# Edge network: who makes the remainders, who copies the selection matrices, and how the two halves of a sum are turned

## The chip, the cores and the metric

The kernel runs on one core of a Trainium2 chip. The metric is the device time of one execution in microseconds (us). The engines are named as the profile names them: PE is TensorE (PEld its weight loads), DVE is VectorE, ACT is ScalarE, POOL is GpSimd, SP issues most of the DMAs. Each has a queue of its own, works it off in order, and waits for the others by semaphores.

## What is computed

Four graph layers, each followed by a residual addition and a layer norm, on 3125 nodes with 64 features and 53125 edges (50000 drawn ones and a loop at each node). The change lies in the second layer, the edge network, whose reference is (cut):

```
row, col = edge_index[0], edge_index[1]
h = concatenate([x[row], edge_attr], axis=1)
h = relu(h @ W1 + b1)
h = h @ W2 + b2
agg = scatter_mean(h, col, x.shape[0])
g = relu(concatenate([x, agg], axis=1) @ W3 + b3)
return g @ W4 + b4
x = _layernorm(x + ...)
```

## The kernel before

The nodes are cut into 25 tiles of 125 (NT), and each tile of destinations has 26 blocks (SB) of 128 edge slots. For a tile the kernel needs the 128 hidden values of every edge, after the relu, summed by destination. That is the stage "edge2", the functions pe_edge2, act_edge2, dve_edge2, pool_edge2 and sp_edge2. It is walked in steps, 7 for each tile, so 175 (G7). A step treats 4 blocks, 512 columns; the seventh step of a tile (g = 6) treats the 2 that are left, 256 columns, and is "the short step". All engines run the same loop over steps, each in its own order:

- **PE** gathers the source nodes' part of the hidden values by multiplying with a selection matrix (L3022, 12 bf16 matmuls in a step, 6 in the short one; three pieces of bf16 stand for one fp32 value). Three steps later (LAG) it sums that step's hidden values by destination (L3035, 4 matmuls, 2 in the short step). Its moving operand has 256 columns: 128 of the rounded value and 128 of the remainder, so the sum comes out in two halves of 128 columns, in bank 4 or 5. Five steps after a tile's last step (LAG + TURN_SUM) it turns the tile's sum (L3043).
- **DVE** adds the edges' part to what PE gathered (L3216, out of PSUM into one of three buffers pre). It makes the selection matrix of the next tile once per tile, in step g = 1 (L3193, src_tables). It makes the remainder, the relu of pre less its rounded value, in the steps g = 1, 3, 5 (L3199, rest). Once a tile it adds the two halves of the sum (L3234, tensor_reduce into `both`), and one step later than the turn it scales the turned sum (L3242).
- **ACT** takes the relu and rounds it to the reduced fp32 that the sum matmul reads (L3144, into one of four act_two). In the steps whose remainder POOL makes it takes the same relu once more, not rounded, into `whole` (L3150).
- **POOL** subtracts the rounded from the whole value in the steps g = 0, 2, 4, 6 (L3109).
- hot_e holds the selection matrix by destination in the sum's format, four buffers. The copy into it is made by POOL in the steps 0, 2, 3, 4, 6 (L3099) and by ACT in the steps 1 and 5 (L3153).

PE waits before each sum for the copy, for ACT's relu, and for the remainder of that step. DVE waits before each addition for the gather. Between these steps lies work once for every four tiles (a chunk, CH = 4, seven in all): two matmuls at the hidden layer (L3053, L3054), the output layer (L3062), four transposes (L3071), the attention inputs (L3080), and on DVE the layer norm (L854 to L861, L928, L929), each at a fixed distance in steps.

The tables that say who does what are REST_BY_POOL and CAST_BY_ACT. SP reloads the inputs of a tile when the copies and the additions of the tile two before it are done.

Of the kernel before, what the change touches and what calls it, by code (L numbers as in the profile page):

```python
# [13 lines left out]
ACT = mybir.ActivationFunctionType  # L14
AX = mybir.AxisListType.X
# [5 lines left out]
HID = 128  # L21
# [4 lines left out]
NP_, NT = 125, 25  # L26
# [122 lines left out]
def build(nc, I, out):  # L149
# [23 lines left out]
    with ExitStack() as ctx:  # L173
# [4 lines left out]
        ident = sb("ident", [128, 128])  # L178
# [31 lines left out]
        y1 = sb("y1", [128, N + WIN])  # L210
# [94 lines left out]
        pre = [e2_at([128, 4 * HID]) for _ in range(2)]  # L305
        low_end, high_end = e1_at.at, e2_at.at
        pre.append(e2_at([128, 4 * HID]))
        whole = [y1[:, (13 + 4 * k) * HID:(17 + 4 * k) * HID] for k in range(2)]
        both = [y1[0:NP_, (11 + k) * HID:(12 + k) * HID] for k in range(2)]
        ln1_sq = y1[0:NP_, 0:13 * C].rearrange("p (i f) -> p i f", f=C)  # L310
        px_rest = [y1[0:NP_, 13 * C + 4 * HID * k:13 * C + 4 * HID * (k + 1)] for k in range(2)]
        m_act = [y1[:, k * CH * NP_:(k + 1) * CH * NP_] for k in range(2)]
# [119 lines left out]
        def bank(b, n=BANK, off=0):  # L432
            return ps[:, b * BANK + off:b * BANK + off + n]
# [6 lines left out]
        def sem(name):  # L440

            if name in sems:
                return sems[name]
            if name not in branch_sems:
                if len(branch_sems) == len(by_branch):
                    by_branch.append(ctx.enter_context(nc.semaphore(f"branch{len(by_branch)}")))
                branch_sems[name] = by_branch[len(branch_sems)]
            return branch_sems[name]
# [18 lines left out]
        V, A, M = nc.vector, nc.scalar.activation, nc.tensor.matmul  # L467
# [2352 lines left out]
        G7 = 7 * NT  # L2820
        LAG = 3
        TURN_SUM = 2
        REST_BY_POOL = (0, 2, 4, 6)
        CAST_BY_ACT = (1, 5)

        def hi(ap):

# [173 lines left out]
        def pe_edge2(pe):  # L3001
# [11 lines left out]
            for step in range(E_STEPS):  # L3013
                if step < G7:
                    d, g = divmod(step, 7)
# [10 lines left out]
                if LAG <= step < G7 + LAG:  # L3026
                    s = step - LAG
                    d, g = divmod(s, 7)
# [10 lines left out]
                d, at = divmod(step - LAG - TURN_SUM, 7)  # L3039
                if at == 0 and 1 <= d <= NT:  # L3040
                    d -= 1
                    pe.wait_ge(sem("both_added"), d + 1)
                    nc.tensor.transpose(bank(4 + d % 2, NP_, 2 * HID), both[d % 2], ident[0:NP_, 0:NP_])\  # L3043
                        .then_inc(sem("sum_turned"), 1)
                for c in range(NCH):
                    if step == hid_step(c):
                        to = bank(6, chunk(c) * NP_)
# [7 lines left out]
                    if step == hid_step(c) + OUT:  # L3055
# [5 lines left out]
                        for j, t in enumerate(tiles(c)):  # L3061
                            ins = M(bank(7, C, j * C)[0:NP_, :], m_act[c % 2][:, j * NP_:(j + 1) * NP_], w4[:, :],  # L3062
                                    start=True, stop=True, skip_group_check=True)
# [28 lines left out]
        def cast_hot(engine, op, s, name):  # L3092

            d, g = divmod(s, 7)
            js = groups(d)[g]
            engine.wait_ge(sem(f"hot_back{d % 2}"), hot_landed(d, 0))
            if s >= NE:
                engine.wait_ge(sem("act_summed"), s - NE + 1)
            op(hot_e[s % NE][:, 0:len(js), :], hot_in[d % 2][:, js[0]:js[0] + len(js), :]).then_inc(sem(name), 1)  # L3099
# [21 lines left out]
        def act_edge2(act):  # L3121
            act_px_mid(act, 0)
            act_back(act, 4)
            act_px_mid(act, 1)
            act_px_high(act, 2)
            ln1_root(act, 2)
            act_px_high(act, 3)
            act_back(act, 5)
            act_px_mid(act, 2)
            act_px_high(act, 4)  # L3130
            act_px_mid(act, 3)
            act_back(act, 6)
            for i in range(5, NCH):
                act_px_high(act, i)
                act_px_mid(act, i - 1)
            act_px_mid(act, NCH - 1)
            for step in range(E_STEPS):
                if step < G7:
                    d, g = divmod(step, 7)
                    m = HID * len(groups(d)[g])  # L3140
                    act.wait_ge(sem("e1_added"), step + 1)
                    if step >= 4:
                        act.wait_ge(sem("act_summed"), step - 3)
                    ins = A(act_two[step % 4][:, 0:m // HID, 0, :],  # L3144
                            pre[step % 3][:, 0:m].rearrange("p (k h) -> p k h", h=HID), ACT.Relu)
                    if g in REST_BY_POOL:
                        n = rests(step, True)
                        if n > 2:
                            act.wait_ge(sem("rest_pool"), n - 2)
                        ins = A(whole[n % 2][:, 0:m], pre[step % 3][:, 0:m], ACT.Relu)  # L3150
                    ins.then_inc(sem("act_relued"), 1)
                    if g in CAST_BY_ACT:
                        cast_hot(act, lambda to, of: A(to, of, ACT.Copy), step, "hot_act")  # L3153
                for c in range(NCH):
                    if step == hid_step(c) + 1:
                        act.wait_ge(sem("m_hid"), c + 1)
                        if c >= 2:
                            act.wait_ge(sem("m_out"), c - 1)
                        A(m_act[c % 2][:, 0:chunk(c) * NP_], bank(6, chunk(c) * NP_), ACT.Relu,
                          bias=prm[:, P_L1B3:P_L1B3 + 1]).then_inc(sem("m_relu"), 1)  # L3160
                    at = slice(c * CH, c * CH + chunk(c))
                    if step == hid_step(c) + ROOT:
                        ln_root(act, c, LN2 + c + 1)
                    if step == hid_step(c) + TURNED:
                        act.wait_ge(sem("back"), NCH + c + 1)
                        A(xt[:, cols(c)], bank(6, chunk(c) * NP_)[0:C, :], ACT.Copy).then_inc(sem("back_ev"), 1)
                    if step == hid_step(c) + HIGH:
                        act.wait_ge(sem("tab_mm"), NCH + c + 1)
                        A(p3[:, at, 0, :], hup_bank(c), ACT.Copy).then_inc(sem("tab_high"), 1)
                    if step == hid_step(c) + MID:  # L3170
                        act.wait_ge(sem("tab_left"), NCH + c + 1)
                        A(p3[:, at, 1, :], hup_left(c), ACT.Copy).then_inc(sem("tab_mid"), 1)

        def dve_edge2(dve, chain):
# [30 lines left out]
            for step in range(E_STEPS):  # L3205
                if step < G7:
                    d, g = divmod(step, 7)
# [15 lines left out]
                if step == 3:  # L3223
                    dve.wait_ge(sem("back_ev"), NCH)
                    V.tensor_tensor(xn[:, :, :], xn[:, :, :], b4b[:, :].unsqueeze(1).to_broadcast([NP_, NT, C]), ALU.add)\
                        .then_inc(sem("x_b4"), 1)
                d, at = divmod(step - LAG - 1, 7)
                if at == 0 and 1 <= d <= NT:
                    d -= 1
                    dve.wait_ge(sem("act_summed"), 7 * d + 7)  # L3230
                    if d >= 2:
                        dve.wait_ge(sem("sum_turned"), d - 1)
                    got = bank(4 + d % 2, 2 * HID)[0:NP_, :]
                    V.tensor_reduce(both[d % 2], got.rearrange("p (t h) -> p h t", t=2), AX, ALU.add).then_inc(sem("both_added"), 1)  # L3234
                d, at = divmod(step - LAG - TURN_SUM - 1, 7)
                if at == 0 and 1 <= d <= NT:
                    d -= 1
                    dve.wait_ge(sem("sum_turned"), d + 1)
                    c, k = divmod(d, CH)
# [10 lines left out]
                for c in range(NCH):  # L3250
                    if step == hid_step(c) + EVICT:
# [3 lines left out]
                        at = slice(c * CH, c * CH + chunk(c))  # L3255
# [4 lines left out]
                    at = slice(c * CH, c * CH + chunk(c))  # L3260
# [781 lines left out]
```

## Time and profile before

| | us |
|---|---|
| median of 3 runs | 1653.72 |
| lowest and highest | 1652.78, 1654.42 |
| profiled execution, its own time | 1656.8 |
| its span in the profile | 1655.0 |
| the stage that the change touches, from 765 to 1050 us | 285 |

The profiled execution was 3.1 us longer than the median. Between 0 and 765 us the edges are sorted and the first layer is computed; after 1050 us come the attention layer and the relation layer. Readings of a row "L3022 ... x12" are a run of 12 instructions with the time from the start of the first to the end of the last. Matmuls overlap and an instruction of DVE or ACT overlaps the next one at its end, so what an engine needs for one is the distance to the start of the next where it did not wait.

### The profile page before, as it was taken

What the parts mean: (1) busy time and instruction counts of PE and PEld (TensorE: products, weight loads), DVE (VectorE), ACT (ScalarE), POOL (GpSimd) and SP (SyncE); (2) the same over time, 40 slices, a digit from 0 to 9 for tenths busy, and PEclk for the clock granted to TensorE, in tenths of its full rate; (3) what the DMA queues carried; (4) which work ended last, traced back from release to release, by engine and by line L of the source; (5) the groups of instructions that cost most, each with busy time, mean ns of one, the idle gap of its engine ahead of it and who ended that gap; (6) DMA issues with size and microseconds to landing.
All of it is one profiled execution on the core that took longest, in us unless ns stands there. A gap on an engine that the chain in (4) does not pass through costs nothing.

```text
span 1655.0 us, 46737 instructions
## 1 busy us (share of the span) xinstructions
PE 1256.5 (76%) x19204; PEld 1134.4 (69%) x19205; DVE 1072.6 (65%) x2449; ACT 814.5 (49%) x2162; POOL 669.5 (40%) x733
## 2 busy tenths in 40 slices
PE   5764452626263689997988888789999989989896
PEld 2653342525252568996878777679999988889896
DVE  8333332425252543467878888688888878978886
ACT  5053442525252532115766666456666657555554
POOL 2777777777777700003878777200100100000000
PEclk9566665767666689997999999899999997999998
DMA  6935555747474858355878778466666503445442
GB/s 193 367 120 206 201 203 187 258 170 276 154 291 139 297 222 289 141 221 224 346 295 314 301 296 314 166 252 236 241 228 233 209 27 138 167 165 193 153 176 81
DMA packets 86125, 359.59 MB, mean 217 GB/s; under 512 B 23740, under 2 KB 35281, under 8 KB 78929
## 3 DMA queue, kind: packets, MB, share of 16 engines
q1 hardware_dynamic: 72594, 348.83, 57.2%
q0 software_dynamic: 13312, 7.69, 1.8%
q8 instruction: 155, 2.54, 0.6%
q14 instruction: 64, 0.52, 0.1%
HBM read 250.77 MB, written 105.68 MB: 215 GB/s over the span
## 4 chain that ended last, share of the span: by engine, by line
PE 35%; POOL 30%; DVE 15%; issue 14%; ACT 4%; DMA 1%; POOLq 0%; DVEq 0%; SPq 0%; ACTq 0%
POOL recs L2192 25%; PE ps L3706 8%; PE ps L2664 6%; PE ps L3352 6%; POOL rounded L3109 4%; PE ps L3720 3%; PE ps L3022 3%; PE ps L3035 2%; POOL rounded L3099 2%; DVE arena L3294 1%; DVE arena L3295 1%; PE ps L3408 1%; ACT arena L3424 1%; PE ps L3337 1%; DVE arena L673 1%
## 5 line engine op out<-in xcount | busy, mean ns | idle before, releaser
L2192 POOL DMA_INDIRECT recs<-arena x416 | 414.0, 995 | 160.3 <-issue 126.0
L2514 PE MATMUL ps<-ident,arena 128*128 128x128 f32 (+1 forms) x175 | 47.5, 419 | 240.6 <-DVE arena L2381 182.3
L2375 DVE TENSOR_TENSOR arena<-arena 128x25 f32<-128x25 int32 x25 | 5.0, 199 | 310.5 <-DMA arena<-recs 274.0
L2514 PEld LDWEIGHTS ps<-ident,arena 128*128 128x128 f32 (+1 forms) x175 | 32.4, 212 | 248.9 <-issue 242.6
L3706 PE MATMUL ps<-arena 125*128 125x64 bf16 x5850 | 192.2, 194 | 11.1 <-issue 10.9
L3706 PEld LDWEIGHTS ps<-arena 125*128 125x128 bf16 x5850 | 186.3, 98 | 13.8 <-issue 13.6
L3752 ACT ACTIVATE arena<-ps,arena 128x64 f32<-128x64 f32 x650 | 141.6, 334 | 102.8 <-PE ps L3720 102.6
L3099 POOL CAST rounded<-arena 128x512 fp32r<-128x512 bf16 (+1 forms) x125 | 95.1, 778 | 167.3 <-DMA arena<-hot_out 163.1
L3109 POOL TENSOR_TENSOR rounded<-y,rounded 128x512 fp32r<-128x512 f32 x100 | 130.2, 1302 | 75.9 <-ACT y L3150 75.8
L3144 ACT ACTIVATE rounded<-arena 128x512 fp32r<-128x512 f32 (+1 forms) x175 | 104.7, 598 | 98.2 <-DVE arena L3216 97.3
L3022 PE MATMUL ps<-arena 125*128 125x128 bf16 x1950 | 145.9, 227 | 4.2 <-DVE arena L3193 4.2
L3035 PE MATMUL ps<-rounded 128*128 128x256 f32 x650 | 124.2, 312 | 30.5 <-POOL rounded L3109 29.9
L3216 DVE TENSOR_TENSOR arena<-ps,arena 128x512 f32<-128x512 f32 (+1 forms) x175 | 112.5, 648 | 38.7 <-PE ps L3022 36.5
L3352 PE MATMUL ps<-arena,y 128*68 128x125 f32 x984 | 123.0, 276 | 10.3 <-ACT y L3434 5.0
L3022 PEld LDWEIGHTS ps<-arena 125*128 125x128 bf16 x1950 | 121.2, 103 | 13.6 <-issue 7.2
L2664 PE MATMUL ps<-agg,arena 125*128 125x193 bf16 (+1 forms) x1250 | 124.6, 253 | 5.3 <-DVE yn L2682 4.9
L2547 ACT ACTIVATE arena<-arena 128x832 f32<-128x832 f32 x25 | 22.4, 898 | 197.1 <-DMA arena<-recs 197.0
L3035 PEld LDWEIGHTS ps<-rounded 128*128 128x128 f32 x650 | 92.4, 198 | 36.0 <-issue 35.6
L3352 PEld LDWEIGHTS ps<-arena,y 128*68 128x68 f32 x984 | 107.2, 143 | 13.5 <-issue 13.1
L2664 PEld LDWEIGHTS ps<-agg,arena 125*128 125x128 bf16 x1250 | 107.6, 101 | 11.4 <-issue 9.9
L2584 ACT ACTIVATE arena<-ps 128x512 f32<-128x512 f32 (+1 forms) x192 | 83.8, 522 | 41.9 <-PE ps L2539 41.9
L2403 DVE TENSOR_TENSOR arena<-iota,iota_i 128x768 bf16<-128x768 bf16 (+1 forms) x150 | 99.8, 735 | 0.9
(392 smaller groups left out, 2717.8 us busy)
## 6 DMA issues: line engine op xcount, KB each, us to landing
arena<-ids_out SPq DMA_DIRECT2D x100, 832.0 KB, 6.4
arena<-hot_out SPq DMA_DIRECT2D x75, 832.0 KB, 4.8
arena<-e_out SPq DMA_DIRECT2D x25, 1664.0 KB, 8.6
arena<-adj_out SPq DMA_DIRECT2D x41, 800.0 KB, 7.9
e_out<-arena SPq DMA_DIRECT2D x25, 1024.0 KB
hot_out<-arena SPq DMA_DIRECT2D x25, 832.0 KB
adj_out<-arena SPq DMA_DIRECT2D x25, 800.0 KB
e_out<-arena SPq DMA_DIRECT2D x25, 640.0 KB
```

Of the source, the lines that this page charges most:

```text
L2192: nc.gpsimd.indirect_dma_start(out=recs, out_offset=bass.IndirectOffsetOnAxis(ap=slot_row[:, t:t + 1], axis=0), in_=rec_in[:, t, :], in_of ...
L2403: ins = V.tensor_tensor(to[d % 2][:, a:b, :].rearrange("p j (n t) -> p j n t", t=2), steps, twice[d % 2][:, kind, a:b, :].unsqueeze(2).to_ ...
L2664: ins = M(to, blocks[0:NP_, k, :], yp[l % 2][:, k, 0:PIECES * C + (l == 0)], start=k == 0, stop=k == NT - 1, skip_group_check=True)
L3022: ins = M(bank(step % 4, HID, k * HID), src_hot[d % 2][0:NP_, j * SLOTS:(j + 1) * SLOTS], px[:, block_of(d, j), piece, :], start=piece == ...
L3035: ins = M(bank(4 + d % 2, 2 * HID), hot_e[s % NE][:, k, :], act_two[s % 4][:, k, :, :].rearrange("p t h -> p (t h)"), start=j == 0, stop=j ...
L3099: op(hot_e[s % NE][:, 0:len(js), :], hot_in[d % 2][:, js[0]:js[0] + len(js), :]).then_inc(sem(name), 1)
L3109: nc.gpsimd.tensor_tensor(act_two[r % 4][:, 0:n, 1, :], whole[rests(r, True) % 2][:, 0:n * HID].rearrange("p (k h) -> p k h", h=HID), act_ ...
L3144: ins = A(act_two[step % 4][:, 0:m // HID, 0, :], pre[step % 3][:, 0:m].rearrange("p (k h) -> p k h", h=HID), ACT.Relu)
L3216: V.tensor_tensor(pre[step % 3][:, 0:m], bank(step % 4, m), e1_in[d % 2][:, 4 * g * HID:4 * g * HID + m], ALU.add).then_inc(sem("e1_added" ...
L3352: ins = M(bank(6 + d % 2, NP_)[0:ROW, :], xmsg[n % 3][:, k, :], hot32[(7 * d + j // 4) % NH][:, j % 4, 0:NP_], start=j == 0, stop=j == NT, ...
L3706: ins = M(bank(step % 4, C, k * C), hot_r[d % 2][r][0:NP_, j * SLOTS:(j + 1) * SLOTS], px3[:, block_of(d, j), piece, r * C:(r + 1) * C], s ...
L3752: ins = A(xrel[q % 3][:, 0, k, :], bank(q % 4, C, k * C), ACT.Copy, scale=w_all[:, d, j:j + 1])
```

## The change

REST_BY_POOL shrinks from the steps 0, 2, 4, 6 to step 6 alone, so DVE makes the remainder in the steps 0 to 5. CAST_BY_ACT goes from 1 and 5 to 0, 1, 3, 4, so POOL keeps the copies of the steps 2, 5 and 6. DVE no longer adds the two halves of a tile's sum; ACT copies both halves out of PSUM into `both`, now 256 wide, and PE turns each half by an ordinary fp32 matmul with the identity, the second one accumulating on the first. The buffers `whole` and `both` move within y1.

```
-        whole = [y1[:, (13 + 4 * k) * HID:(17 + 4 * k) * HID] for k in range(2)]
-        both = [y1[0:NP_, (11 + k) * HID:(12 + k) * HID] for k in range(2)]
+        whole = [y1[:, (16 + 4 * k) * HID:(20 + 4 * k) * HID] for k in range(2)]
+        both = [y1[0:NP_, (8 + 2 * k) * HID + 512:(10 + 2 * k) * HID + 512] for k in range(2)]
...
-        REST_BY_POOL = (0, 2, 4, 6)
-        CAST_BY_ACT = (1, 5)
+        REST_BY_POOL = (6,)
+        CAST_BY_ACT = (0, 1, 3, 4)
...
                     pe.wait_ge(sem("both_added"), d + 1)
-                    nc.tensor.transpose(bank(4 + d % 2, NP_, 2 * HID), both[d % 2], ident[0:NP_, 0:NP_])\
+                    to = bank(4 + d % 2, NP_, 2 * HID)
+                    M(to, both[d % 2][:, 0:HID], ident[0:NP_, 0:NP_], start=True, stop=False)
+                    M(to, both[d % 2][:, HID:2 * HID], ident[0:NP_, 0:NP_], start=False, stop=True)\
                         .then_inc(sem("sum_turned"), 1)
...
                     if g in CAST_BY_ACT:
                         cast_hot(act, lambda to, of: A(to, of, ACT.Copy), step, "hot_act")
+                d, at = divmod(step - LAG - 1, 7)
+                if at == 0 and 1 <= d <= NT:
+                    d -= 1
+                    act.wait_ge(sem("act_summed"), 7 * d + 7)
+                    if d >= 2:
+                        act.wait_ge(sem("sum_turned"), d - 1)
+                    A(both[d % 2], bank(4 + d % 2, 2 * HID)[0:NP_, :], ACT.Copy).then_inc(sem("both_added"), 1)
...
-                d, at = divmod(step - LAG - 1, 7)
-                if at == 0 and 1 <= d <= NT:
-                    d -= 1
-                    dve.wait_ge(sem("act_summed"), 7 * d + 7)
-                    if d >= 2:
-                        dve.wait_ge(sem("sum_turned"), d - 1)
-                    got = bank(4 + d % 2, 2 * HID)[0:NP_, :]
-                    V.tensor_reduce(both[d % 2], got.rearrange("p (t h) -> p h t", t=2), AX, ALU.add).then_inc(sem("both_added"), 1)
```

The engines' queues at the same places, first before, then after. In the changed kernel the line numbers are higher: on DVE L3225 is the addition of L3216, L3208 the remainder of L3199, L3202 the selection matrix of L3193, and L3243 the scaling of L3242.

PE before, from one turn on: the turn, then the gather of the short step.

```order
L3043 MATMUL ps<-ident,y 128x125
L3022 MATMUL ps<-arena 128x128 x6
L3035 MATMUL ps<-rounded 128x256 x4
L3022 MATMUL ps<-arena 128x128 x12
L3035 MATMUL ps<-rounded 128x256 x4
L3022 MATMUL ps<-arena 128x128 x12
```

PE after, at the same place:

```order
L3044 MATMUL ps<-ident,y 128x125
L3045 MATMUL ps<-ident,y 128x125
L3022 MATMUL ps<-arena 128x128 x6
L3035 MATMUL ps<-rounded 128x256 x4
L3022 MATMUL ps<-arena 128x128 x12
L3035 MATMUL ps<-rounded 128x256 x4
L3022 MATMUL ps<-arena 128x128 x12
```

The turn is two matmuls now, and the rest of PE's order stands.

DVE before, from the scaling of one tile's sum (in step 6) to the reduction of the next:

```order
L3242 TENSOR_TENSOR agg<-ps,arena 128x125
L3216 TENSOR_TENSOR arena<-ps,arena 128x512 x2
L3193 TENSOR_SCALAR arena<-arena,pidx_f 128x3328
L3216 TENSOR_TENSOR arena<-ps,arena 128x512
L3199 SCALAR_TENSOR_TENSOR rounded<-arena,rounded 128x4x128
L3216 TENSOR_TENSOR arena<-ps,arena 128x512 x2
L3199 SCALAR_TENSOR_TENSOR rounded<-arena,rounded 128x4x128
L3234 TENSOR_REDUCE y<-ps 125x128
```

DVE after, at the same place:

```order
L3243 TENSOR_TENSOR agg<-ps,arena 128x125
L3225 TENSOR_TENSOR arena<-ps,arena 128x512 x2
L3208 SCALAR_TENSOR_TENSOR rounded<-arena,rounded 128x4x128
L3202 TENSOR_SCALAR arena<-arena,pidx_f 128x3328
L3225 TENSOR_TENSOR arena<-ps,arena 128x512
L3208 SCALAR_TENSOR_TENSOR rounded<-arena,rounded 128x4x128
L3225 TENSOR_TENSOR arena<-ps,arena 128x512
L3208 SCALAR_TENSOR_TENSOR rounded<-arena,rounded 128x4x128
L3225 TENSOR_TENSOR arena<-ps,arena 128x512
L3208 SCALAR_TENSOR_TENSOR rounded<-arena,rounded 128x4x128
```

A remainder now follows every addition of 512 columns, one of them ahead of the selection matrix, and the reduction is gone.

ACT after, one tile from its step 0 on. L3146 is the relu, L3155 the copy, L3162 the new copy of the sum, L3152 the relu into whole.

```order
L3146 ACTIVATE rounded<-arena 128x4x128
L3155 ACTIVATE rounded<-arena 128x512
L3146 ACTIVATE rounded<-arena 128x4x128
L3155 ACTIVATE rounded<-arena 128x512
L3146 ACTIVATE rounded<-arena 128x4x128 x2
L3155 ACTIVATE rounded<-arena 128x512
L3146 ACTIVATE rounded<-arena 128x4x128
L3155 ACTIVATE rounded<-arena 128x512
L3162 ACTIVATE y<-ps 125x256
L3146 ACTIVATE rounded<-arena 128x4x128
L3146 ACTIVATE rounded<-arena 128x2x128
L3152 ACTIVATE y<-arena 128x256
```

The copy of the sum stands behind the relu and the copy of step 4; before, ACT had no part in it.

## Rows read from the trace of the kernel before

**Rows 1.** Windows: length, busy (count) of PE PEld DVE ACT POOL, PE clock, DMA.

```profile
765.00:1050.00 285.00, 246.26 (x2757) 223.07 (x2757) 240.34 (x391) 184.00 (x351) 219.46 (x224) 0.95 0.74 286
...
970.00:975.00 5.00, 1.98 (x27) 1.74 (x27) 4.96 (x8) 3.55 (x7) 3.18 (x3) 1.00 1.04 441
```

**Rows 2.** Waits from 790 to 1040 us: in total, times, longest.

```profile
DVE arena L3216 <- PE ps L3022: 32.0, 44, 2.1
...
PE ps L3035 <- POOL rounded L3109: 26.5, 25, 3.0
```

**Rows 3.** Groups by line and form, 765 to 1050 us: busy, mean ns | idle before.

```profile
L3199 DVE SCALAR_TENSOR_TENSOR rounded<-arena,rounded 128x512 fp32r<-128x512 f32 x75 | 70.7, 942 | 4.3 <-ACT rounded L3144 3.1
```

**Rows 4.** Timeline of DVE, the reductions that mark tiles: start, length, instruction.

```profile
898.00 0.41 DVE L3234 TENSOR_REDUCE y<-ps 125x128 f32<-125x256 f32 x1
907.71 0.41 DVE L3234 TENSOR_REDUCE y<-ps 125x128 f32<-125x256 f32 x1
...
953.09 0.41 DVE L3234 TENSOR_REDUCE y<-ps 125x128 f32<-125x256 f32 x1
```

**Rows 5.** Timeline of all engines, a quiet tile: one that has no chunk work.

```profile
898.46 0.33 PE L3043 MATMUL ps<-ident,y 125*128 125x125 f32 x1 [0.22 <-DVE y L3234]
...
898.62 0.50 PE L3022 MATMUL ps<-arena 125*128 125x128 bf16 x6
898.93 0.72 PE L3035 MATMUL ps<-rounded 128*128 128x256 f32 x4
...
899.49 0.84 PE L3022 MATMUL ps<-arena 125*128 125x128 bf16 x12
...
900.15 0.73 PE L3035 MATMUL ps<-rounded 128*128 128x256 f32 x4
...
901.60 0.69 DVE L3216 TENSOR_TENSOR arena<-ps,arena 128x512 f32<-128x512 f32 x1
...
902.21 1.08 DVE L3193 TENSOR_SCALAR arena<-arena,pidx_f 128x3328 bf16<-128x3328 f16 x1
902.33 0.63 ACT L3144 ACTIVATE rounded<-arena 128x512 fp32r<-128x512 f32 x1
902.45 1.96 POOL L3109 TENSOR_TENSOR rounded<-y,rounded 128x512 fp32r<-128x512 f32 x1 [0.53 <-ACT y L3150]
...
902.86 0.62 ACT L3153 ACTIVATE rounded<-arena 128x512 fp32r<-128x512 bf16 x1
...
903.20 0.69 DVE L3216 TENSOR_TENSOR arena<-ps,arena 128x512 f32<-128x512 f32 x1
903.80 1.16 DVE L3199 SCALAR_TENSOR_TENSOR rounded<-arena,rounded 128x512 fp32r<-128x512 f32 x1
```

**Rows 6.** Timeline, other places: a remainder alone, and a selection matrix beside a copy.

```profile
885.87 0.68 DVE L3199 SCALAR_TENSOR_TENSOR rounded<-arena,rounded 128x512 fp32r<-128x512 f32 x1
...
869.36 1.51 DVE L3193 TENSOR_SCALAR arena<-arena,pidx_f 128x3328 bf16<-128x3328 f16 x1
869.38 0.61 POOL L3099 CAST rounded<-arena 128x512 fp32r<-128x512 bf16 x1 [0.20 <-PE ps L3035]
```

**Rows 7.** Timeline of PE: ordinary fp32 matmuls, two records each.

```profile
894.84 0.99 PE L3080 MATMUL ps<-watt,xt_rows 66*125 66x74 f32 x8
```

**Rows 8.** The chain of work that ended last: chunk matmuls at the hidden layer.

```profile
866.10 1.11 PE ps L3053 x2
867.20 0.84 PE ps L3054 x2
```

**Rows 9.** Timeline of DVE, the middle of a chunk's layer norm.

```profile
877.83 0.41 DVE L857 TENSOR_TENSOR yn<-yn,stat 125x256 f32<-125x256 f32 x1
...
879.15 0.69 DVE L3216 TENSOR_TENSOR arena<-ps,arena 128x512 f32<-128x512 f32 x1
879.76 0.41 DVE L860 TENSOR_REDUCE stat<-y 125x4 f32<-125x256 f32 x1
...
880.31 0.69 DVE L3216 TENSOR_TENSOR arena<-ps,arena 128x512 f32<-128x512 f32 x1
```

## The prediction, before the changed kernel ran

> **What bounds the kernel now.** I read the windows first. In the 285 us of the stage from 765 to 1050 us PE is busy for 246.3 us, DVE for 240.3, POOL for 219.5 and ACT for 184.0 [rows 1]. No engine is full, so what counts is who waits for whom. The waits name a ring: from 790 to 1040 us PE waits 26.5 us for POOL's remainder before a sum, and DVE waits 32.0 us for PE's gather before an addition [rows 2]. A late remainder delays the sum, the sum delays the next gather behind it on PE, and the gather delays DVE. The timeline says what a tile takes: a quiet one 9.71 us (from the reduction at 898.00 to that at 907.71), four tiles with one chunk's work 45.38 us (907.71 to 953.09) [rows 4]. I therefore lay out one tile's longest loop after the change and compare it with these two numbers. Outside the stage nothing changes, and what lies behind it shifts with its end.
>
> **Prices.** They are distances from the start of one instruction to the next where nothing waited. PE: 12 gather matmuls 0.66 (899.49 to 900.15), 6 of them 0.31, 4 sum matmuls 0.56 (898.93 to 899.49), today's turn 0.16 [rows 5]; DVE sees a gather 0.84 us after its first matmul, about 0.89 with the semaphore. DVE: an addition 0.61 (901.60 to 902.21), the selection matrix 0.99 (902.21 to 903.20); ACT starts its relu 0.73 after the addition starts (901.60 to 902.33), and its next instruction 0.53 later [rows 5]. A remainder alone takes 0.68 us, as an addition does, so 0.60 to its successor [rows 6].
>
> **POOL's work moves to DVE.** For each tile DVE gets three more remainders of 512 columns, 75 in all, 75 x 0.60 = 45 us. It loses 25 reductions of 0.41 us each, about 0.33 in distance, 8 us. What gets cheaper is the waiting at POOL. The remainder that starts at 903.80 takes 1.16 us: POOL's subtraction, begun at 902.45, ends at 904.41, and 0.55 us later the remainder ends too [rows 5]. So a remainder stands until POOL is through. On average it takes 0.942 us [rows 3] against 0.68, so 75 x 0.26 = 20 us. DVE's busy time becomes 240 + 45 - 8 - 20 = 257 us, under the stage's length, but now the highest.
>
> The Trainium skill (SBUF — State Buffer, Who interferes with whom) states this as a rule: VectorE with two inputs in SBUF and GpSimd reading SBUF share a port pair that is locked for a whole instruction, and the later one blocks. The trace agrees, as just read. Taken as all that limits this stage, it gives the first rival below.
>
> **ACT** loses 75 whole relus of 512 columns and gains 50 copies of the same size and 25 copies of 256 columns out of PSUM, taken at 0.41 us (the reduction reads the same bank in that time [rows 4]). It stays near 180 of 285 us, so no load; but its new copy of the sum stands behind the relu and the copy of step 4, and PE's turn waits for it. Behind the turn stand the gather of the short step and everything after it.
>
> **The two turns.** The trace has no ordinary fp32 matmul of 125 columns. Eight records, four matmuls, of 74 columns took 0.99 us, 0.12 each [rows 7], and two records of 500 columns 0.84 us [rows 8], 0.42 each or 0.105 for 125 columns. So weight loading and issue set the pace, and I take four records at 0.12, 0.48 us. Below, it can't be less than two turns as they are now, 0.32; above, I take 0.75, an estimate: one and a half times the 0.12 for each record, for a first weight load that nothing hides and 125 columns in place of 74. No gain is possible here, since both matmuls do what one did.
>
> The Trainium skill speaks against this edit: TensorE: Matmul & The Clock Gate, Terms, calls transpose mode four times faster for fp32. By that the two ordinary matmuls would take 2 x 4 x 0.16 = 1.28 us, and the forecast would lie 25 x 0.8 = 20 us higher; the rows of ordinary matmuls in this trace speak for the smaller price.
>
> **The loop of a quiet tile after the change**, each item waiting for the one before it, with its g and ' for the next tile. On PE: the two turns 0.48, gather of g 6 0.31, sum of g 3 0.56, gather of 0' 0.66, sum of g 4 0.56, gather of 1' 0.89 until DVE starts: 3.46. On DVE: addition 1' 0.61, remainder 0' 0.60, selection matrix 0.99, addition 2', remainder 1', addition 3', remainder 2' 2.42, addition 4' 0.73 until ACT starts: 5.35. On ACT: relu 4' 0.53, copy 4' 0.53, copy of the sum 0.41 and its semaphore 0.05: 1.52. Together 10.33 us. One wait comes on top. POOL's copy for 2' becomes free when the sum of g 5 has run, 0.5 to 0.6 us after the addition 1' began, just when the remainder 0' has taken the port. The copy then goes next and the selection matrix waits for it. Rows 6 show that pair: begun together with a copy of 0.61 us, the matrix took 1.51 us in place of 1.08. I take 0.4, so 10.7 us against 9.7: **+1.0 us for a quiet tile**. The bounds of this wait are 0 and 0.61.
>
> Why not shorter, though POOL's subtractions are gone? Because PE now gets the sum one step later. Today DVE's reduction follows its remainder 3' at once and PE waits 0.22 us for it [rows 5]; then it will wait about 1.6 us in each tile: remainder 2' done, PE needs 0.56 for the sum of g 2', while ACT delivers the copy only 0.73 + 0.53 + 0.53 + 0.46 = 2.25 us after addition 4' began. Meanwhile DVE has queued work for 1.8 us and then stands until the gather of g 6 arrives.
>
> **Four tiles with a chunk.** On the loop lie, once per chunk, the hidden matmuls, 1.11 + 0.84 = 1.95 us [rows 8], between the sum of g 4 and the gather of 1'; the four transposes, 4 x 0.16 = 0.6 at most, I take 0.5; and part of the layer norm. That takes 1.32 us (877.83 to 879.15) and 0.55 (879.76 to 880.31) [rows 9] on DVE between additions 6 and 1'. From the end of the short gather's issue DVE then needs 0.2 until it sees it, then the short addition 0.34 and later the scaling 0.20 (both estimates, by their columns from the addition's 0.61), a remainder 0.60, the layer norm 1.32, addition 0' 0.61 and the norm's 0.55, in all 3.82, where PE needs 0.56 + 0.66 + 0.56 + 0.89 = 2.67: 1.15 more. Four tiles: 4 x 10.7 + 1.95 + 0.5 + 1.15 = 46.4 against 45.4, **+1.0 us**. It is less than four quiet tiles would lose, because today's chunk tiles lose time to POOL that comes back: PE is busy for only 1.98 of the 5 us from 970 to 975 [rows 1].
>
> **Sum.** The first three distances between tiles are quiet, 3 x 1.0 = 3 us; five groups of four follow, 5 x 1.0 = 5; the first tile and the last one, which only drain, about 1. Together +9 us. The profiled execution would go from 1656.8 to 1665.8; it stood 3.1 us over the median, so the median becomes **1662.7 us**, 0.5% slower. The edits' bounds: the port wait -10 to +5, the turns (0.32 and 0.75) -4 to +7, prices of the hand-laid chunks some 5 either way. Unlikely all on one side; I take 1651 to 1676 as the forecast's own range.
>
> **Rivals.**
> 1. *The port was the bound, DVE is now.* If PE runs far enough ahead that the late sum hides, the stage lasts as long as DVE's 257 us and about 4 to start, 24 us less: 1630 us. For it: 26.5 us of PE's waits on POOL go for certain [rows 2]. Against: the order puts the short gather behind the turn. It decides if the copy of the sum comes within about 0.6 us after PE could take it (DVE's queued 1.8 us, less the sum 0.56, the turns 0.48 and the short gather's first part), where the hand layout has 1.6. Half of it, with DVE waiting in some tiles only, gives 1640.
> 2. *It evens out.* Without the port wait (POOL's copy loses to the selection matrix) a quiet tile takes 10.3 and four with a chunk 44.8: +2 - 3 + 1, 1654 us, no change.
> 3. *The clock falls.* PE stands once more per tile, for 1.6 us. Should the granted clock drop for it, gathers take twice as long, about 1.5 us a tile: 1700 us. Against it, PE stood about 3 us between 970 and 975 and the clock stayed at 1.00, 2.4 GHz [rows 1].
> 4. *Only the fp32 price is wrong*, the turns taking 1.28 us: 1683 us.
>
> **Chances.** Forecast 0.62, rival 1 0.13, rival 2 0.14, rival 3 0.03, rival 4 0.08. A measurement of this kernel can tell about 0.2%, 3.3 us. The lower edge of the forecast's range and rival 2 share "same": slower 0.68, same 0.15, faster 0.17. For 8 in 10 the range covers the forecast's own and rival 2 and goes toward rival 4 and the half case of rival 1: 1645 to 1680 us.
>
> **What the new profile would show.** The distance between scalings in quiet tiles 10.7 us; PE waiting for ACT's copy about 35 us in all, and hardly for POOL; DVE's wait for the gather still 30 us or more, DVE busy for about 257 us; remainders at 0.7 to 0.75 us on average; the selection matrix near 1.45 us; four records of the turn in 0.48 us. Wrong would be: PE's wait for the copy under 0.6 us a tile (rival 1), a selection matrix at 1.08 us (rival 2), a clock under 0.9 in the stage (rival 3), or turns over 1 us (rival 4).

## The result and the profile after

| | before, us | after, us |
|---|---|---|
| median of 17 runs each | 1653.39 | 1659.51 |
| ratio, with its 95% interval | | 1.0033 (1.0019 to 1.0047) |
| span of the profiled execution | 1655.0 | 1656.6 |
| from the first to the last scaling of a tile's sum | 261.09 | 265.02 |
| a quiet tile (one without chunk work) | 9.70 | 10.67 |
| four tiles with a chunk's work, the second to the fourth of the five groups | 45.33, 45.37, 45.17 | 45.80, 45.80, 45.79 |

The change makes the kernel slower by 0.33%, about 5.5 us by the ratio. The forecast was 1663 us, 9 us slower.

The first view is the windows of the kernel after, the stage and the stretch that answers to the second of [rows 1]; the columns are those of [rows 1].

```profile
765.00:1050.00 285.00, 239.71 (x2813) 220.13 (x2814) 255.12 (x437) 179.01 (x349) 72.23 (x99) 0.99 0.78 287
...
970.00:975.00 5.00, 4.39 (x61) 4.04 (x59) 4.87 (x11) 2.51 (x6) 1.49 (x2) 1.00 0.94 362
```

POOL fell from 219.5 to 72.2 us and DVE rose from 240.3 to 255.1. PE, which stood for 3 us in the second stretch before, is busy for 4.39 of its 5 us now. From 790 to 1045 us it nowhere stands for longer than 1.24 us, and the stage still ends later. The waits from 790 to 1045 us, as in [rows 2], say for what:

```profile
PEld ps L3044 <- ACT y L3162: 31.0, 22, 1.4
PE ps L3044 <- ACT y L3162: 26.5, 22, 1.2
DVE arena L3225 <- PE ps L3022: 22.0, 26, 2.1
...
PE ps L3035 <- ACT rounded L3146: 8.2, 12, 0.8
```

No sum waits for POOL any more. PE waits 26.5 us for ACT's copy of the sum (L3162) ahead of the turn (L3044) instead; that the total is the same as before is chance, for these are 22 waits of 1.2 us and those were 25 of up to 3.0. The groups by line and form, 765 to 1060 us, answer to [rows 3]:

```profile
L3208 DVE SCALAR_TENSOR_TENSOR rounded<-arena,rounded 128x512 fp32r<-128x512 f32 x150 | 102.3, 682 | 0.0
...
L3202 DVE TENSOR_SCALAR arena<-arena,pidx_f 128x3328 bf16<-128x3328 f16 x25 | 33.4, 1335 | 0.0
...
L3162 ACT ACTIVATE y<-ps 125x256 f32<-125x256 f32 x25 | 9.1, 365 | 0.0
```

Twice as many remainders, and each takes 682 ns on average in place of 942: they no longer stand behind POOL, and only one of the 150 took more than 0.75 us. The selection matrix takes 1335 ns on average. The end of one tile and the loop's next turn, in the timeline of all engines (the tile takes 10.67 us like a quiet one, though two short DVE instructions of a chunk lie in it):

```profile
898.32 0.68 DVE L3208 SCALAR_TENSOR_TENSOR rounded<-arena,rounded 128x512 fp32r<-128x512 f32 x1
...
898.92 0.68 DVE L3225 TENSOR_TENSOR arena<-ps,arena 128x512 f32<-128x512 f32 x1
898.97 0.61 ACT L3155 ACTIVATE rounded<-arena 128x512 fp32r<-128x512 bf16 x1
899.49 0.36 ACT L3162 ACTIVATE y<-ps 125x256 f32<-125x256 f32 x1
...
899.91 0.49 PE L3044 MATMUL ps<-ident,y 125*128 125x125 f32 x2 [1.21 <-ACT y L3162]
...
900.46 0.50 PE L3022 MATMUL ps<-arena 125*128 125x128 bf16 x6
...
900.99 0.42 DVE L3225 TENSOR_TENSOR arena<-ps,arena 128x256 f32<-128x256 f32 x1 [0.79 <-PE ps L3022]
...
904.04 0.68 DVE L3208 SCALAR_TENSOR_TENSOR rounded<-arena,rounded 128x512 fp32r<-128x512 f32 x1
904.06 1.13 POOL L3101 CAST rounded<-arena 128x512 fp32r<-128x512 bf16 x1 [1.07 <-PE ps L3035]
...
904.63 1.43 DVE L3202 TENSOR_SCALAR arena<-arena,pidx_f 128x3328 bf16<-128x3328 f16 x1
```

The loop can be read off: the copy in step 4 (898.97), behind it the copy of the sum (899.49), PE's turns after 1.21 us of waiting (899.91), 0.55 us for the four records, the short gather at 900.46, and DVE, idle for 0.79 us, adds its two blocks at 900.99. Below it stands the port wait: POOL's copy is issued at 904.06, while the remainder runs; the copy goes next and the matrix behind it takes 1.43 us in place of 1.08.

The scalings of the tiles' sums on DVE mark the tiles as the reductions did in [rows 4]:

```profile
901.93 0.28 DVE L3243 TENSOR_TENSOR agg<-ps,arena 128x125 f32<-128x125 f32 x1
```

In the same view they stand at 912.60, 925.16, 936.66, 947.73 and 958.40: distances of 10.67, 12.56, 11.50, 11.07 and 10.67 us.

### The profile page after: what moved, and what is told of

Its sections match the earlier page's. It is cut to its first block, busy times and chain, and to the rows that moved or that the text cites. A ratio compares the mean times of both kernels' runs of the same rounds, so it can differ in the third digit from the quotient of the medians.

```text
span 1656.6 us, 46841 instructions
## 1 busy us (share of the span) xinstructions
PE 1243.7 (75%) x19279; PEld 1126.2 (68%) x19280; DVE 1087.6 (66%) x2499; ACT 809.7 (49%) x2162; POOL 524.8 (32%) x608
## 4 chain that ended last, share of the span: by engine, by line
PE 36%; POOL 25%; DVE 20%; issue 14%; ACT 4%; DMA 1%; POOLq 0%; DVEq 0%; ACTq 0%; SPq 0%
POOL recs L2192 25%; PE ps L3707 9%; PE ps L2664 6%; PE ps L3353 6%; PE ps L3721 3%; DVE rounded L3208 3%; PE ps L3022 3%; DVE arena L3225 3%; PE ps L3035 2%; DVE arena L3295 1%; DVE arena L3296 1%; PE ps L3409 1%; ACT arena L3425 1%; DVE arena L673 1%; PE ps L3338 1%
## 5 line engine op out<-in xcount | busy, mean ns | idle before, releaser
L3707 PEld LDWEIGHTS ps<-arena 125*128 125x128 bf16 x5850 | 186.9, 99 | 14.4 <-issue 14.0
L3146 ACT ACTIVATE rounded<-arena 128x512 fp32r<-128x512 f32 (+1 forms) x175 | 104.9, 600 | 105.7 <-DVE arena L3225 104.2
L3101 POOL CAST rounded<-arena 128x512 fp32r<-128x512 bf16 (+1 forms) x75 | 53.8, 717 | 317.0 <-DMA arena<-hot_out 162.4
L3022 PE MATMUL ps<-arena 125*128 125x128 bf16 x1950 | 139.9, 221 | 4.2 <-DVE arena L3202 4.2
L3225 DVE TENSOR_TENSOR arena<-ps,arena 128x512 f32<-128x512 f32 (+1 forms) x175 | 113.4, 648 | 29.2 <-PE ps L3022 25.0
L3035 PE MATMUL ps<-rounded 128*128 128x256 f32 x650 | 120.0, 304 | 15.4 <-ACT rounded L3146 11.9
L3022 PEld LDWEIGHTS ps<-arena 125*128 125x128 bf16 x1950 | 114.7, 99 | 13.2 <-issue 7.2
L3208 DVE SCALAR_TENSOR_TENSOR rounded<-arena,rounded 128x512 fp32r<-128x512 f32 x150 | 102.3, 682 | 0.0
L3035 PEld LDWEIGHTS ps<-rounded 128*128 128x128 f32 x650 | 88.7, 190 | 18.8 <-issue 18.7
```

What stands on the lines that cost most here:

```text
L3022: ins = M(bank(step % 4, HID, k * HID), src_hot[d % 2][0:NP_, j * SLOTS:(j + 1) * SLOTS], px[:, block_of(d, j), piece, :], start=piece == ...
L3035: ins = M(bank(4 + d % 2, 2 * HID), hot_e[s % NE][:, k, :], act_two[s % 4][:, k, :, :].rearrange("p t h -> p (t h)"), start=j == 0, stop=j ...
L3146: ins = A(act_two[step % 4][:, 0:m // HID, 0, :], pre[step % 3][:, 0:m].rearrange("p (k h) -> p k h", h=HID), ACT.Relu)
L3208: V.scalar_tensor_tensor(out=act_two[s % 4][:, 0:n, 1, :], in0=pre[s % 3][:, 0:n * HID].rearrange("p (k h) -> p k h", h=HID), scalar=0.0, ...
L3225: V.tensor_tensor(pre[step % 3][:, 0:m], bank(step % 4, m), e1_in[d % 2][:, 4 * g * HID:4 * g * HID + m], ALU.add).then_inc(sem("e1_added" ...
L3707: ins = M(bank(step % 4, C, k * C), hot_r[d % 2][r][0:NP_, j * SLOTS:(j + 1) * SLOTS], px3[:, block_of(d, j), piece, r * C:(r + 1) * C], s ...
```

## The experiments

Times of runs are medians of 6 to 12 runs beside the kernel before on the same chip (of 17 for the change itself), and the ratios are to it. The kernel before took 1655.5 us beside e1 to e4, 1652.6 beside e5 to e7 and 1655.4 beside e8 to e10, so kernels of different rows are compared by their ratios and not by their medians. The last four columns are from one profiled execution each: the distance from the first to the last scaling of a tile's sum, the median of the first three distances between tiles, which are quiet, and a third of the stretch from the eighth to the twentieth scaling, three times four tiles with a chunk's work. The last column is what four such tiles take where the granted clock stays at 1.00 (of the first four of the five groups). In a group with a fall of the clock, 0.92 to 0.96 as its mean, they take up to 2.1 us longer, so a difference in "first to last" or "four tiles" can be one of the clock.

| kernel | median | ratio (interval) | first to last | quiet tile | four tiles | at clock 1.00 |
|---|---|---|---|---|---|---|
| before | | 1 | 261.1 | 9.70 | 45.3 | 45.2 |
| after | 1659.5 | 1.0033 (1.0019 to 1.0047) | 265.0 | 10.67 | 45.8 | 45.8 |
| e1 split only | 1651.8 | 0.9980 (0.9962 to 0.9999) | 256.9 | 9.76 | 44.3 | 44.3 |
| e2 turn only | 1657.2 | 1.0008 (0.9986 to 1.0029) | 265.0 | 10.11 | 46.0 | 45.3 |
| e3 after, turn later | 1652.1 | 0.9984 (0.9965 to 1.0002) | 257.6 | 9.79 | 43.9 | 43.6 |
| e4 before, turn later | 1642.0 | 0.9921 (0.9899 to 0.9943) | 250.0 | 9.82 | 42.4 | 42.3 |
| e5 after, copy of the sum first | 1649.6 | 0.9975 (0.9961 to 0.9988) | 256.8 | 10.14 | 44.4 | 44.4 |
| e6 after, copies 1 and 2 exchanged | 1653.7 | 0.9999 (0.9984 to 1.0014) | 259.7 | 10.31 | 44.9 | 44.9 |
| e7 split only, turn later | 1644.3 | 0.9942 (0.9920 to 0.9963) | 251.2 | 9.48 | 43.3 | 42.6 |
| e8 e3, e5 and e6 together | 1644.6 | 0.9935 (0.9913 to 0.9958) | 248.7 | 9.12 | 42.8 | 42.4 |
| e9 e7 with copies 1 and 2 exchanged | 1643.9 | 0.9936 (0.9913 to 0.9959) | 253.3 | 9.14 | 43.9 | 42.6 |
| e10 e4 again | 1643.2 | 0.9929 (0.9902 to 0.9955) | 251.7 | 10.06 | 42.9 | 42.3, 42.7 |

**The two halves of the change apart.** e1 keeps the new tables and takes the turn back:

```
-                    A(both[d % 2], bank(4 + d % 2, 2 * HID)[0:NP_, :], ACT.Copy).then_inc(sem("both_added"), 1)
...
+                    got = bank(4 + d % 2, 2 * HID)[0:NP_, :]
+                    V.tensor_reduce(both[d % 2][:, 0:HID], got.rearrange("p (t h) -> p h t", t=2), AX, ALU.add).then_inc(sem("both_added"), 1)
...
-                    M(to, both[d % 2][:, 0:HID], ident[0:NP_, 0:NP_], start=True, stop=False)
-                    M(to, both[d % 2][:, HID:2 * HID], ident[0:NP_, 0:NP_], start=False, stop=True)\
+                    nc.tensor.transpose(bank(4 + d % 2, NP_, 2 * HID), both[d % 2][:, 0:HID], ident[0:NP_, 0:NP_])\
```

> The changed kernel with its new split of remainders and copies, but the sum's two halves are again added by DVE's reduction (0.41 us) and turned by one transpose. Ring theory (the stage's length is the loop remainder 2', ACT's copy of the sum, two turns, short gather, ...): after remainder 2' DVE needs an addition, remainder 3' and the reduction, 1.6 us, where ACT's copy came after about 1.75 us, and the turn falls from 0.55 to 0.16 us, so about 0.6 us less in each tile: quiet tile 10.67 to about 10.0 us, four tiles 45.8 to about 43.5, total 1659.5 to about 1648. Load theory (DVE, busiest with 255 us, sets the end): DVE gets 25 x 0.33 = 8 us more, 1667. If the new split alone costs the time (port wait), it stays at 1659.

The new split alone is faster than before, 0.9980, by a margin barely clear of the noise (0.9962 to 0.9999), and clearly faster than the changed kernel (1.0019 to 1.0047). Its stage is 4.2 us shorter than before and 8.1 us shorter than after the change, with more work on DVE (264.4 us busy from 765 to 1050 us in place of 255.1). That ends the load theory: DVE was busy longer and the end came earlier. The waits of e1, 790 to 1040 us, show that PE's wait before the turn is the reduction's now, and about half as long:

```profile
PE ps L3043 <- DVE y L3234: 14.8, 23, 0.7
```

The quiet tile fell by 0.91 us rather than the 0.6 expected: 0.39 from the turns, 0.5 from that wait. Four tiles came to 44.3 us and the runs to 1651.8, both less of a gain than the 43.5 and 1648 expected. Against the kernel before, the split gains in the groups, 44.3 us against 45.2 at the full clock; a quiet tile took 9.76 us against 9.70.

e2 keeps the new turn and takes the tables back:

```
-        REST_BY_POOL = (6,)
-        CAST_BY_ACT = (0, 1, 3, 4)
+        REST_BY_POOL = (0, 2, 4, 6)
+        CAST_BY_ACT = (1, 5)
```

> The kernel before with its old split, but ACT copies the two halves of the sum and PE turns them by two matmuls. Ring theory: PE's turn waits up to 1 us longer and takes 0.4 us more, DVE loses 0.33 us a tile; in this kernel POOL's subtraction still delays the sums, so part of it hides: quiet tile 9.7 to about 10.1 us, total 1653 to 1658. Load theory: DVE has 8 us less to do, 1645.

The quiet tile is 10.11 us, as the ring gives it, though DVE had less to do than before (231.5 in place of 240.3 us). The stage of the profiled execution is 3.9 us longer than before, but not all of that can be put down to the turn: 1.3 us are in the first three tiles, and of the first four groups the one at a granted clock of 1.00 took 45.3 us, against 45.2 before, while the three in which the clock fell took 46.2 to 46.4. The runs put e2 at 1.0008, an interval that holds both no change and 0.3%. So the price of the new turn is shown on top of the new split, by after against e1 (1.0033 to 0.9980); with the old split it isn't shown by the runs.

**The turn's place.** With TURN_SUM = 2 the turn stands in step g = 5 of the next tile, ahead of the short gather; with 3 it stands in g = 6, behind it. The step in which a chunk's work starts is reckoned from the same number (hid_step adds LAG + TURN_SUM + 2), so the hidden matmuls, the layer norm and the rest come one step later too. e3 is the changed kernel, e4 the kernel before, each with one number changed:

```
-        TURN_SUM = 2
+        TURN_SUM = 3
```

> The changed kernel with TURN_SUM 3 in place of 2: PE's two turns, and all that hangs on them, stand one step later, behind the short gather. Ring theory: PE's wait for ACT's copy (28 us) nearly goes, the short gather no longer stands behind the turn; quiet tiles are then held by DVE itself (13 instructions, about 10.6 us with the port wait), so they stay near 10.6, but four tiles with a chunk fall from 45.8 to about 44: total 1659.5 to about 1649. Load theory: same work on DVE, no change, 1659.

> The kernel before with TURN_SUM 3 in place of 2, nothing else. Ring theory: the short gather no longer stands behind the turn there either; DVE's 32 us of waits for the gather shrink by about 10 and those of POOL for ACT with them: quiet tile 9.7 to about 9.3 us, four tiles 45.4 to about 42, total 1653 to about 1636. If POOL's subtractions with their port waits bound the old kernel alone, no change, 1653.

Both are faster than the kernel that they edit, e3 with 0.9984 against 1.0033 and e4 with 0.9921 against 1, and both by less than expected (1652.1 us where 1649 was expected, 1642.0 where 1636 was). In e3 PE hardly waits for ACT's copy (3.7 us on the weight loads in place of 31.0), DVE for the gather 9.6 us in place of 22.0. A quiet tile fell further than expected, to 9.79 us; the shortest between chunk work take 10.2 to 10.4. The first three tiles have no chunk work, so the 0.88 us that each of them gained comes from the turn's place, with the scaling behind it. e4, which touches nothing of the change, is the fastest kernel of the first four: the short gather stood behind the turn there too, and DVE's wait for the gather halved from the 32.0 us of [rows 2]. Its waits, 790 to 1040 us:

```profile
PE ps L3035 <- POOL rounded L3109: 16.2, 29, 1.1
DVE arena L3216 <- PE ps L3022: 15.5, 40, 1.1
```

But the ring's reason for it isn't shown. Its quiet tiles, expected at 9.3 us, gained nothing (9.46, 9.82 and 10.03 us against 9.70 before). The gain lies in the groups with chunk work, 42.3 us against 45.2 at the full clock, and there PE's longest stand, 3.0 us for POOL's remainder in each group, became 1.2. The edit moves the chunk's work as well as the turn, and no run parts the two, so which of them gives these 2.9 us a group stays open.

**The copy of the sum on ACT.** In e5 it stands ahead of the copy of step 4:

```
                     ins.then_inc(sem("act_relued"), 1)
+                d, at = divmod(step - LAG - 1, 7)
+                if at == 0 and 1 <= d <= NT:
...
+                    A(both[d % 2], bank(4 + d % 2, 2 * HID)[0:NP_, :], ACT.Copy).then_inc(sem("both_added"), 1)
...
                     if g in CAST_BY_ACT:
                         cast_hot(act, lambda to, of: A(to, of, ACT.Copy), step, "hot_act")
```

> The changed kernel, but in step 4 ACT copies the two halves of the sum before it copies the selection matrix, not after. Same instructions, only their order on ACT. Ring theory: PE's wait for the copy of the sum (1.2 us a tile) falls by the 0.53 us of the copy ahead of it, the quiet tile from 10.67 to about 10.15 us, total 1659.5 to about 1649. Load theory (DVE's 255 us set the end): no change, 1659.

This is the cleanest of the tests, since every engine has the same instructions. The quiet tile went from 10.67 to 10.14 us, by the 0.53 us of one instruction on ACT, and the kernel from 1.0033 to 0.9975 of the kernel before, intervals that don't touch. PE's wait for the copy in the timeline of e5 is now 0.7 us a tile, from 1.21:

```profile
896.85 0.36 ACT L3160 ACTIVATE y<-ps 125x256 f32<-125x256 f32 x1
...
897.26 0.49 PE L3044 MATMUL ps<-ident,y 125*128 125x125 f32 x2 [0.67 <-ACT y L3160]
```

**The port wait.** e6 exchanges two copies between ACT and POOL:

```
-        CAST_BY_ACT = (0, 1, 3, 4)
+        CAST_BY_ACT = (0, 2, 3, 4)
```

> The changed kernel with the copies of steps 1 and 2 exchanged: ACT makes 0, 2, 3, 4, POOL 1, 5, 6. Every engine has as much to do as before the exchange, but POOL's copy is no longer ready just before DVE's selection matrix. Port-wait theory: the selection matrix goes from 1.43 back to 1.08 us, and since it is on the loop the quiet tile goes from 10.67 to about 10.3 us, total 1659.5 to about 1651. If the port wait is hidden behind another wait, the matrix gets shorter and the tile doesn't, 1659.

The selection matrix is back at its own time, in the groups by line and form of e6:

```profile
L3202 DVE TENSOR_SCALAR arena<-arena,pidx_f 128x3328 bf16<-128x3328 f16 x25 | 27.1, 1082 | 0.0
```

and the quiet tile went from 10.67 to 10.31, by the 0.36 us that the matrix lost. So the port wait lies on the loop and is worth 0.36 us in a quiet tile; four tiles with a chunk, where three of the four matrices stood behind a copy, fell by 0.9. The runs went from 1.0033 to 0.9999 of the kernel before.

**Together.** e7 is e1 with TURN_SUM 3, e8 the changed kernel with the edits of e3, e5 and e6, e9 is e7 with the exchange of e6, and e10 is e4 once more beside e8 and e9.

> The new split with DVE's reduction and one transpose, as in the split-only run, and the turn one step later (TURN_SUM 3). Ring theory: PE's 15 us of waits for the reduction go; what is left is DVE's own work plus the port wait, quiet tile 9.76 to about 9.6, four tiles from 44.25 to about 42.5 us, total 1651.8 to about 1644. It should come near the kernel before with the same turn (1642) if the split itself is about neutral, and well behind it if DVE's added 45 us of remainders then set the end.

> The changed kernel with all three single edits: turn one step later, ACT's copy of the sum ahead of its copy in step 4, and the copies of steps 1 and 2 exchanged. Ring theory: once the turn stands a step later PE no longer waits for the copy, so the order on ACT adds little; the selection matrix falls to 1.08 us, worth 0.36 us in a tile that DVE itself holds. Four tiles from 43.6 (turn later alone) to about 42.7, total 1652 to about 1647. If the three gains simply added up it would be 1659.5 - 7 - 10 - 6 = 1637.

> The new split, DVE's reduction and one transpose, turn one step later, and the copies of steps 1 and 2 exchanged. Ring theory: four tiles 42.5 to about 41.8, total 1644 to about 1641. It is the best form of the new split that I can build; if it is no better than the kernel before with the later turn (1642), the split is worth nothing and the turn's place is all.

> The kernel before with the turn one step later, a second time, so that it stands beside the two others on one chip. 1642 again, four tiles 42.3 us.

In e9 the three groups of four differ, 44.6, 44.5 and 42.5 us, with the granted clock, which was 0.92, 0.92 and 1.00 in them; e7's 42.6, 44.7 and 42.5 us go with 1.00, 0.92 and 1.00. The single gains don't add up: e8 came to 1644.6, not 1637. The gains are those of one loop, and once the turn is off it, other waits hold the tiles; which ones was not worked out. e7, e8, e9, e4 and e10 end at 1644.3, 1644.6, 1643.9, 1642.0 and 1643.2 with overlapping intervals, so once the turn stands late enough it can't be told which split of the remainders is the better one. In e9 the selection matrix fell from 1181 to 1078 ns on average. The quiet tile followed, 9.48 to 9.14 us, but four tiles with a chunk at the full clock did not, 42.6 us in both, nor did the runs, 0.9942 and 0.9936, where 1641 us and 41.8 us were expected; the port wait is worth something only where it is on the loop. The lowest ratios of the study are those of the kernel before with TURN_SUM = 3, 0.9921 and 0.9929, from a change of one digit.

## Why the prediction was right, and where its sizes were off

- **The ring and its quiet tile.** Laid out as 10.33 us and a port wait of 0.4, together 10.7; measured 10.67. This was the forecast's core, and e5 and e6 take two of its items away, each for its own size (0.53 and 0.36 us). That the total fits to 0.1 us is partly luck, since its items were off both ways (the turns 0.07 us too cheap, the copy of the sum 0.41 us against 0.36).
- **The turns.** Taken at 0.48 us, measured 0.55. The price from the ordinary fp32 matmuls of [rows 7] and [rows 8] held roughly. It was read with the end of the last matmul in it: from start to start the eight records of 74 columns took 0.83 us (894.84 to 895.67), 0.10 each, and the four of the turn 0.14 each.
- The Trainium skill's figure for transpose mode, four times faster for fp32 (TensorE: Matmul & The Clock Gate, Terms), read as a price for the pair gave an estimate of 1.28 us; the trace doesn't bear that out, 0.55 for four records against 0.16 for the one they replace, 1.7 times for each turn. From 74 to 125 columns, 1.7 times as many, a record went from 0.10 to 0.14 us, so the columns are only a part of what is paid for.
- **PE's wait for the copy.** Forecast about 1.6 us a tile and 35 in all; it was 1.21 and 26.5 from 790 to 1045 us. ACT delivered as laid out (addition 4' at 897.72, PE's turn at 899.91, 2.19 us, forecast 2.25). PE was ready later: the sum of step 2' began at 897.98, 0.26 us after that addition and not 0.11, and its last matmul ended after 0.72 us, where I had counted the 0.56 to the next start.
- **DVE's load.** Forecast 257 us, measured 255.1 in the same window. Remainders forecast at 0.7 to 0.75, measured 0.68. The matrix took 1.43 us in the 18 tiles in which a copy started ahead of it and 1.08 in the other 7, forecast near 1.45.
- **The mis-sized term: four tiles with a chunk.** Forecast 46.4 against 45.4, measured 45.8, so +0.4 to +0.6 in place of +1.0. The items can be read as the excess of the group's tiles of 12.57, 11.49 and 11.08 us over 10.67: the tile with the hidden matmuls 1.90 (forecast 1.95), that with the layer norm 0.82 (1.15), that with the transposes 0.41 (0.5).
- **A gain that I had not counted.** The forecast took 45.4 us for each of the five groups before. The first took 46.64 us (819.12 to 865.76), for PE had stood and then the granted clock from 835 to 840 us was 0.61, the mean of a stretch at 2.4 and one at 1.2 GHz; the 12 gather matmuls at 837.62 took 1.50 us in place of 0.84. After the change the group took 45.81 us, 0.8 less, and the clock there was 1.00. The two windows, before and after:

```profile
835.00:840.00 5.00, 3.37 (x21) 3.22 (x22) 3.47 (x6) 2.54 (x7) 4.84 (x5) 0.61 1.00 421
```

```profile
835.00:840.00 5.00, 3.52 (x46) 3.10 (x45) 4.93 (x10) 3.03 (x6) 0.61 (x1) 1.00 0.90 349
```

  The forecast's argument that the clock stays up rested on the one stand from 970 to 975 us. PE stood as long for POOL in each of the five groups, and after four of the stands the clock fell (windows of 5 us behind them at 0.61 to 0.83); the one that I had read is the exception. The first and the fourth, before:

```profile
836.63 1.19 PE L3035 MATMUL ps<-rounded 128*128 128x256 f32 x4 [3.01 <-POOL rounded L3109]
...
973.99 0.71 PE L3035 MATMUL ps<-rounded 128*128 128x256 f32 x4 [3.02 <-POOL rounded L3109]
```

  The change takes all five stands away, and the clock in the stage went from 0.95 to 0.99. So by the trace the stage's 3.9 us are 2.9 for the first three tiles and 1.1 for the five groups, where I had 3 and 5, and the start and the end, taken at 1, cost nothing.
- **The rivals.** Rival 1 (POOL was the bound) was half right: without the new turn (e1) the split does gain, 0.2%, not the 24 us of the rival. Rival 2 had its reason wrong: the port wait did come. The measured time lies between its 1654 us and the forecast because four tiles with a chunk lost 0.4 to 0.6 us and not 1.0. Rivals 3 and 4 fell, by the clock of 0.99 and the 0.55 us.

The stage in the profiled execution is 3.9 us longer and the span 1.6, while the runs' ratio gives 5.5 us. The 3.9 lies inside the interval (3.1 to 7.8 us). The span differs less because in the profiled execution after the change the first scaling came 1.0 us earlier and what follows the last one was 1.3 us shorter, in parts of the program that the change doesn't touch. The two profiled executions also stand differently to their medians, that of the kernel before 3.4 us over it and that of the changed kernel 1.1 under, so one pair of spans can't size a change of 5 us.

## What to carry to other kernels

When a program's engines take turns, price an edit by the loop it stands on and not by the engine it relieves: here 147 us of work left POOL and the kernel became slower, because the sum of a tile now came from a copy that stood behind another on ACT, the turn that waits for it had doubled, and PE's next gather stood behind that turn. Look what is queued behind a waiting instruction first; in the changed kernel, moving the waiting instruction one step later (0.5%) was worth about as much as moving the copy that it waits for one place ahead (0.6%), and either was worth more than the split had gained (0.2%). An edit of one digit can move more than its name says, as TURN_SUM moved the chunk's work; keep a stretch without that work to tell the two apart. Read every place of a kind before arguing from one: four of five like stands had a fall of the clock behind them. And before taking work off an engine that waits a lot, ask for which instruction on the loop its buffers, its port or its queue position was the cause.

## What the runs showed of the hardware

- In 18 tiles of the changed kernel a GpSimd copy, itself held up by a remainder, started 0.57 to 0.61 us ahead of the selection matrix; it took 1.12 to 1.16 us and the matrix 1.43 to 1.44. In the 7 tiles without a copy there the matrix took 1.08 to 1.09. That agrees with the Trainium skill (SBUF — State Buffer, Who interferes with whom: issue order decides who blocks). In the kernel before, five copies started 0.01 to 0.02 us behind the matrix, as in [rows 6]; they took their usual 0.61 us and the matrix 1.50 to 1.51, so at that distance the recorded starts don't tell who blocks.
- The tiles of the changed kernel repeat to 0.01 us, the first three at 10.66 or 10.67 us and the first four groups at 45.79 to 45.81, where the kernel before had 45.2 to 46.6 us for the same four. The granted clock was 1.00 in each group, with a stand of PE of 1.1 to 1.2 us in each tile.
- The length of PE's stand alone doesn't tell whether the clock falls. Behind five stands of 3.0 us in the kernel before it fell four times; behind five pairs of stands of 1.29 and 1.33 us in e7 it fell twice, and a group with such a fall took 43.4 and 44.7 us in place of 42.6.
- An fp32 matmul of 125 columns is two records, each with a weight load of 0.19 us; the first pair of a turn took 0.32 us (899.91 to 900.23) and the second 0.23 (to 900.46).
